# A mixture-of-experts stage between two attentions: when expert codes are read, rows are zeroed, outputs fetched and one batch staged

## What is computed

```python
    x = x + _L0_attn_ref(_layernorm(x, axis=-1), ...)
    x = x + _L0_xattn_ref(_layernorm(x, axis=-1), ctx_1024, ctx_1024, ...)
    x = x + _L0_ffn_ref(_layernorm(x, axis=-1), ...)    # mixture of experts
    x = x + _L1_attn_ref(_layernorm(x, axis=-1), ...)
    x = x + _L1_xattn_ref(_layernorm(x, axis=-1), ctx_1024, ctx_1024, mask_1xSxS2_ff0, ...)
    x = x + _L1_ffn_ref(_layernorm(x, axis=-1), ...)

def _L0_ffn_ref(x, gate_w, gate_b, w1, b1, w2, b2):
    gate_logits = jnp.einsum('bsd,de->bse', x, gate_w) + gate_b
    weights, indices = jax.lax.top_k(gate_logits, TOP_K)          # 2 of 8 experts
    weights = jax.nn.softmax(weights, axis=-1)
    h = jnp.einsum('bsd,edh->ebsh', x, w1) + b1[:, None, None, :]
    xh, gh = jnp.split(h, 2, axis=-1)
    act = jax.nn.silu(gh) * xh
    out_e = jnp.einsum('ebsf,efd->ebsd', act, w2) + b2[:, None, None, :]
    ...
    return jnp.sum(sel * weights[..., None], axis=2)
```

## Time and profile before

| | us |
|---|---|
| median of 3 runs | 814.25 (810.34 to 815.94) |
| the profiled execution, its own time | 816.3 |
| its span, first to last instruction | 814.5 |
| busy in the span: PE, VectorE, ScalarE, GpSimd | 691.9, 554.0, 412.8, 287.2 |
| outputs of the tiles (y_sb), first and last start | 370.7 to 512.5 |
| mean granted clock of TensorE | 0.875 of full speed |

### The profile page before, as it was taken

One profiled execution on the slowest core, in us unless ns is written; L12 is line 12 of the kernel. 1 busy time (PEld: TensorE's weight loads), 2 busy tenths in 40 slices (PEclk: granted clock), 3 DMA queues, 4 the chain that ended last, 5 costly groups with the idle time before them and its releaser, 6 DMA issues.

```text
span 814.5 us, 16187 instructions
## 1 busy us (share of the span) xinstructions
PE 691.9 (85%) x5016; PEld 377.3 (46%) x5021; DVE 554.0 (68%) x1674; ACT 412.8 (51%) x787; POOL 287.2 (35%) x509
## 2 busy tenths in 40 slices
PE   2768999999989999558699897788899989997987
PEld 1334455454434454348599896222232323334543
DVE  3757678787745556637357584797798998943564
ACT  1322565656664544213233354165787777784544
POOL 5732444554551204373123242235233241341310
PEclk9785999999985756759899999588999999999899
DMA  7552443254222311227457767220222101000000
GB/s 220 163 180 84 144 116 109 74 175 157 70 79 69 90 43 50 91 84 209 137 168 227 246 183 257 71 92 27 93 102 94 53 28 53 2 2 1 13 14 27
DMA packets 77252, 83.45 MB, mean 102 GB/s; under 512 B 15040, under 2 KB 67712, under 8 KB 77168
## 3 DMA queue, kind: packets, MB, share of 16 engines
q1 hardware_dynamic: 74896, 77.72, 31.0%
q0 software_dynamic: 2272, 4.69, 1.6%
HBM read 53.99 MB, written 28.00 MB: 101 GB/s over the span
## 4 chain that ended last, share of the span: by engine, by line
PE 58%; DVE 19%; issue 8%; DMA 5%; ACT 3%; SPq 3%; POOL 2%; DVEq 0%; ACTq 0%; POOLq 0%
PE bank_pv L743 12%; DVE mx L603 10%; PE bank_turn L587 8%; PE bank_scores L1827 6%; PE bank_scores L2161 5%; PE bank_scores L695 4%; PE bank_scores L1835 3%; PE bank_turn L762 3%; DMA probs<-routed_tokens 2%; PE bank_turn L804 2%; PE bank_turn L541 2%; DVE stats L463 1%; PE bank_turn L591 1%; PE bank_turn L592 1%; PE bank_scores L1238 1%
## 5 line engine op out<-in xcount | busy, mean ns | idle before, releaser
L603 DVE TENSOR_REDUCE mx<-bank_turn 128x1 f32<-128x512 f32 (+3 forms) x451 | 259.8, 615 | 58.8 <-PE bank_turn L592 31.8
L587 PE MATMUL bank_turn<-stk 64*128 64x77 bf16 (+4 forms) x707 | 166.2, 316 | 29.3 <-DVE mx L603 21.4
L695 PE MATMUL bank_scores<-stk 64*128 64x512 bf16 (+4 forms) x576 | 179.1, 376 | 5.3 <-ACT probs L716 4.0
L720 ACT ACTIVATE probs<-bank_scores 128x1024 f32<-128x1024 f32 (+4 forms) x160 | 117.0, 768 | 109.2 <-PE bank_scores L695 109.0
L716 ACT ACTIVATE probs<-bank_scores 128x512 f32<-128x512 f32 x256 | 138.9, 605 | 37.7 <-PE bank_scores L695 36.9
L743 PE MATMUL bank_pv<-probs,vsl 128*32 128x512 f32 (+4 forms) x1152 | 146.5, 583 | 2.7 <-POOL probs L728 1.8
L587 PEld LDWEIGHTS bank_turn<-stk 64*128 64x128 bf16 x707 | 54.7, 102 | 135.3 <-DVE mx L603 70.8
L1827 PE MATMUL bank_scores<-probs,w 128*128 128x128 f32 x624 | 88.7, 293 | 7.6 <-issue 5.1
L1827 PEld LDWEIGHTS bank_scores<-probs,w 128*128 128x128 f32 x624 | 83.2, 208 | 9.4 <-issue 9.1
L1886 ACT ACTIVATE probs<-bank_scores,b_cols 128x128 f32<-128x128 f32 x156 | 44.6, 368 | 82.0 <-PE bank_scores L1827 81.8
L728 POOL TENSOR_SCALAR_AFFINE_SELECT probs<-probs 128x256 f32<-128x256 f32 x128 | 51.8, 408 | 75.5 <-ACT probs L720 74.2
(11 more groups left out here) (289 smaller groups left out, 988.1 us busy)
## 6 DMA issues: line engine op xcount, KB each, us to landing
w<-in_M_w SPq DMA_DIRECT2D x43, 512.0 KB, 4.4
stk<-stack_A SPq DMA_DIRECT2D x64, 256.0 KB, 3.1
stack_A<-parts SPq DMA_DIRECT2D x16, 384.0 KB, 3.1
stack_A<-fill SPq DMA_DIRECT2D x8, 512.0 KB, 5.2
stack_A<-parts SPq DMA_DIRECT2D x16, 256.0 KB, 3.2
stk<-stack_X SPq DMA_DIRECT2D x16, 256.0 KB, 2.7
probs<-routed_tokens SPq DMA_DIRECT2D x39, 65.0 KB, 2.7
stack_A<-parts SPq DMA_DIRECT2D x16, 128.0 KB, 3.2
```

The source lines that it names most:

```text
L587: mm = e.matmul(o, stk[r, slot, 0, pp, qt * P:(qt + 1) * P], stk[r, slot, 1, pp, 0:keys], start=True, stop=not a.causal)
L603: e.tensor_reduce(o.rearrange("p h q -> p q h"), bank_of((g, m))[:, 0:k * keys].rearrange("p (q h k) -> p q h k", q=len(tiles), h=len(hs)) ...
L695: mm = e.matmul(score_bank(g, kt, i)[0:a.kp, 0:S - q0], stk[r, slot, 1, pp, kt * P:kt * P + a.kp], stk[r, slot, 0, pp, q0:S], start=True, ...
L720: e.activation(probs[0:a.kp, probs_of(g, kt), j:HG:2, 0:n], bank_scores[0:a.kp, 2 * j:2 * j + 2, 0:n], ACT.Exp, scale=1 / math.sqrt(HD)).t ...
```

## The change

It alters where things stand in the five lists; no product and no byte of data is added or left out, but the splitting of batch 1 goes to other engines.

1. `codes` becomes `expert_of`: each engine reads one word where the first tile of its four needs it. It is still 11 reads on each engine.
2. SyncE writes one zero row block after each of tiles 1 to 8 instead of all eight between tiles 1 and 2.
3. The outputs of batches 0 and 1 are fetched from ScalarE's queue, after silu of tile 26 (`fetch_sp` becomes `fetch_dma`).
4. Batch 1 is no longer projected and split beside the tiles. Its combining and normalising stand at tiles 33 to 35; its transposing and projecting stand between the maxima of unit 32 in the second stream, and GpSimd splits q ahead of `neg_of(32)` and k behind it. Batch 0's splitting is spread over tiles 30 to 33, its part 3 made at tile 32 instead of 33, and its `stack_dma` stands after tile 36 instead of 37. Beside tiles 37 and 38 stand 2 maxima each instead of 3, all of them behind `output(37)`, and the fourth bank is free from the start of the second stream.
5. GpSimd writes row blocks 4 and 5 ahead of the norm of batch 2, and 6 and 7 ahead of the norm of batch 3.

```diff
@@ -1407,11 +1401,13 @@
             neg_of(e, 1)
             for g in STREAMS[0]:
                 unit_pool(e, g)
-            norm_pool(e, M0.ln, 2)
             for t in range(QT, QT + 2):
                 scatter_pool(e, t)
+            norm_pool(e, M0.ln, 2)
+            for t in range(QT + 2, 2 * QT):
+                scatter_pool(e, t)
             norm_pool(e, M0.ln, 3)
-            for t in range(QT + 2, NT):
+            for t in range(2 * QT, NT):
                 scatter_pool(e, t)
 
         def first_stream_sp(e):
@@ -1428,12 +1424,21 @@
                 unit_sp(e, g)
 
         def second_stream_pe(e):
+            away[3] = 0
             for k in range(2 * MAXIMA_BESIDE, len(A1.items)):
                 max_pe(e, 32, k)
+                if k == 2 * MAXIMA_BESIDE:
+                    norm_pe(e, A1.ln, 1)
+                elif k % 3 == 0 and k < len(A1.items):
+                    z = (k - 6) // 3
+                    for part in range(2):
+                        if z < 2:
+                            stage_q_pe(e, A1, 1, z, part)
+                        elif z == 2:
+                            stage_v_pe(e, A1, 1, part)
             turn_pe(e, 32)
             for k in range(len(A1.items) // 2):
                 max_pe(e, 33, k)
-            away[3] = 0
             for g in STREAMS[1]:
                 unit_pe(e, g)
             last_layers_pe(e)
@@ -1444,19 +1449,26 @@
             turn_dve(e, 32)
             for k in range(len(A1.items) // 2):
                 max_dve(e, 33, k)
-            part31_dve(e, 1)
             for g in STREAMS[1]:
                 unit_dve(e, g)
             last_layers_dve(e)
 
         def second_stream_act(e):
+            norm_act(e, A1.ln, 1)
+            for z in range(2):
+                stage_q_act(e, A1, 1, z)
+            stage_v_act(e, A1, 1)
             for g in STREAMS[1]:
                 unit_act(e, g)
             last_layers_act(e)
 
         def second_stream_pool(e):
             values_pool(e, 32)
+            for step in range(4):
+                split_pool(e, A1, 1, 0, step)
             neg_of(e, 32)
+            for step in range(4):
+                split_pool(e, A1, 1, 1, step)
             bias_pool(e, A1, 0)
             bias_pool(e, A1, 1)
             for end in (0, S + 1):
...
@@ -1712,18 +1722,16 @@
                     moments_dve(e, A1.ln, 0)
                 elif t == 28:
                     normalise(e, A1.ln, 0)
-                elif t == 29:
+                elif t == 30 or t == 31:
+                    rest1_dve(e, 0, t - 30)
+                elif t == 32:
+                    part31_dve(e, 0)
+                elif t == 33:
                     combine_dve(e, 2, 1)
-                elif t == 30:
+                elif t == 34:
                     moments_dve(e, A1.ln, 1)
-                elif t == 31:
-                    rest1_dve(e, 0)
-                elif t == 32:
+                elif t == 35:
                     normalise(e, A1.ln, 1)
-                elif t == 33:
-                    part31_dve(e, 0)
-                elif t == 36:
-                    rest1_dve(e, 1)
                 elif t > 36:
                     for k in range(MAXIMA_BESIDE * (t - 37), MAXIMA_BESIDE * (t - 36)):
                         max_dve(e, A1.first, k)
@@ -1737,19 +1745,22 @@
             e.wait_ge(m["recip"], 1)
             e.tensor_tensor(gate[:, 1], gate[:, 0], gate_t[:, 1], ALU.mult).then_inc(m["gates"], 1)
 
-        MAXIMA_BESIDE = 3
+        MAXIMA_BESIDE = 2
 
         def place_in(t):
 
             return t if t < EARLY else LATE_AT + t - EARLY
 
-        def codes(e, late):
-
-            e.wait_ge(m["tile_e"], CODED * (1 + late))
-            words = range(LATE_AT // CODED, SLOTS // CODED) if late else range(LATE_AT // CODED)
-            code = {c: e.value_load(tile_e[0:1, c:c + 1], min_val=0, max_val=NE ** CODED - 1) for c in words}
-            tiles = range(EARLY, BUSY_TILES) if late else range(EARLY)
-            return {t: (code[place_in(t) // CODED] >> (3 * (place_in(t) % CODED))) & (NE - 1) for t in tiles}
+        def expert_of(e, ex, t):
+
+            k = place_in(t)
+            if k % CODED == 0:
+                e.wait_ge(m["tile_e"], CODED * (1 + (k >= LATE_AT)))
+                code = e.value_load(tile_e[0:1, k // CODED:k // CODED + 1], min_val=0, max_val=NE ** CODED - 1)
+                for n in range(CODED):
+                    if place_in(t + n) == k + n:
+                        ex[t + n] = (code >> (3 * n)) & (NE - 1)
+            return ex[t]
 
         def combine_dve(e, ln, b):
 
@@ -1858,14 +1868,10 @@
                     norm_pe(e, A1.ln, 0)
                 elif t == 30:
                     stage1_pe(e, 0)
-                elif t == 33:
-                    norm_pe(e, A1.ln, 1)
-                elif t == 34:
-                    stage1_pe(e, 1)
-                elif t > 35:
-                    if t == 36:
+                elif t > 36:
+                    if t == 37:
                         away[:3] = 3 * taken
-                    for k in range(MAXIMA_BESIDE * (t - 36), min(MAXIMA_BESIDE * (t - 35), MAXIMA_BESIDE * 2)):
+                    for k in range(MAXIMA_BESIDE * (t - 37), MAXIMA_BESIDE * (t - 36)):
                         max_pe(e, A1.first, k)
             e.wait_ge(m["y_out"], FREE + BUSY_TILES)
 
...
+            ex = {}
             for t in range(BUSY_TILES):
-                if t == EARLY:
-                    ex |= codes(e, 1)
                 gate_part(t, ex)
-                if t == 30:
+                if t == 26:
+                    for b in range(2):
+                        fetch_dma(e, b)
+                elif t == 30:
                     norm_act(e, A1.ln, 0)
                 elif t == 31:
                     stage1_act(e, 0, 0)
                 elif t == 32:
                     stage1_act(e, 0, 1)
+                    stage1_act(e, 0, 2)
                 elif t == 33:
-                    stage1_act(e, 0, 2)
+                    stage_v_act(e, A1, 0)
                     stage1_act(e, 0, 3)
-                elif t == 34:
-                    norm_act(e, A1.ln, 1)
-                elif t == 35:
-                    stage1_act(e, 1, 0)
-                elif t == 36:
-                    stage1_act(e, 1, 1)
-                    stage1_act(e, 1, 2)
-            stage1_act(e, 1, 3)
 
         def moe_sp(e):
             def tile(t):
@@ -1920,48 +1920,47 @@
                     e.wait_ge(m["y_at"], t - 1)
                 e.dma_start(x_in[:, t % 2], scr_xn[bass.ds(row, P), :]).then_inc(m["tile_in"][t % 2], 16)
 
-            def weights(t, ex):
+            def weights(t):
+                n = expert_of(e, ex, t)
                 wait(e, m["plain_half"], t - W_SLOTS + 1)
-                e.dma_start(w_now[:, t % W_SLOTS], d["M0_w"][bass.ds(ex[t], 1)].rearrange("a p n -> p (a n)"))\
+                e.dma_start(w_now[:, t % W_SLOTS], d["M0_w"][bass.ds(n, 1)].rearrange("a p n -> p (a n)"))\
                     .then_inc(m["w_in"][t % W_SLOTS], 16)
 
+            def zeros(n):
+                if n == 0:
+                    e.wait_ge(m["zero_at"], 1)
+                row = e.value_load(zero_row[0:1, n:n + 1], min_val=0, max_val=DEAD - P)
+                e.dma_start(scr_xn[bass.ds(row, P), :], pads[:, n]).then_inc(m["zeros"], 16)
+
+            ex = {}
             e.wait_ge(m["zeroed"], 2)
             e.dma_start(scr_xn[DEAD:DEAD + 2 * P, :].rearrange("(n p) d -> p n d", p=P), pads[:, NE:PADS])\
                 .then_inc(s_zero, 16)
-            ex = codes(e, 0)
             for t in range(W_SLOTS):
-                weights(t, ex)
+                weights(t)
             e.wait_ge(s["pv"], chunk0[2 * UN])
             e.wait_ge(m["scattered"][0], 16 * 2 * NT // 2)
-            for t in range(2):
-                tile(t)
-            e.wait_ge(m["zero_at"], 1)
-            for n in range(NE):
-                row = e.value_load(zero_row[0:1, n:n + 1], min_val=0, max_val=DEAD - P)
-                e.dma_start(scr_xn[bass.ds(row, P), :], pads[:, n]).then_inc(m["zeros"], 16)
-            for t in range(2, EARLY):
+            for t in range(EARLY):
                 tile(t)
                 if t >= W_SLOTS:
-                    weights(t, ex)
-            ex |= codes(e, 1)
-            weights(EARLY, ex)
+                    weights(t)
+                if t > 0:
+                    zeros(t - 1)
+            weights(EARLY)
             e.wait_ge(s_zero, 16)
             e.wait_ge(m["zeros"], 16 * NE)
             e.wait_ge(m["scattered"][1], 16 * 2 * NT // 2)
             for t in range(EARLY, BUSY_TILES):
                 tile(t)
                 if t > EARLY:
-                    weights(t, ex)
-                if t == 28:
-                    for b in range(2):
-                        fetch_sp(e, b)
-                elif t == 37:
+                    weights(t)
+                if t == 36:
                     for z in range(2):
```

(2 more changed lines are left out.)

44 lines of the change are left out of this document (17 added, 27 removed).

## The result

The changed kernel takes 789.77 us (median of 5 runs, 789.07 to 795.67) where the kernel before takes 815.66 (5 runs beside it, 810.34 to 815.96): ratio 0.9728, 95% interval 0.9686 to 0.9770. The forecast was 792. The profiled execution is the longest of the five, 795.67, against 816.3 before: 20.6 us less.

The account below looks back on a forecast made before the run. PE bounds undisturbed tiles at 2.84 us each, so gains lie where PE waits. Terms -4.5 - 11.7 - 2 - 4.9 + 1 = -22.1 took the 814.25 us median to 792; range 782 to 803.

Parts of the forecast that it names:

- Start: First tiles: reads no longer block VectorE and PE (3.95 us), tile 2 in time (0.57); -4.5, bounds -2 to -5.5.
- Tiles 7 to 10: Single reads end the serial waits; tile 9 still about 1.7 us late for zero blocks; -11.7, bounds -13.4 to -8.
- Fetches: Fetches from ScalarE's queue let the tile go ahead, though transfers are shared; -2, bounds -4.3 to +1.
- Tiles 33 to 38: Batch 1's projections and waits go; new 4.1 us wait at tile 37, 0.8 slower clock; -4.9, bounds -9 to -1.
- Behind the tiles: Second stream: more maxima and batch 1's staging, part 3 dropped, q's splitting covered; +1, bounds -0.7 to +4.
- Reads that stand open on PE: In the tile loop, PE's nine later words cost 0.65 us each, 5.9 us: 798; chance 0.11.
- The tail gives it back: Tile 37's wait grows, tail gains nothing, `neg_of(32)` waits behind q's splitting at half clock: 800; chance 0.14.
- No new waits: Tiles 9 and 37 arrive in time, another 1.7 + 4.9 us: 785; chance 0.08.
- The slower case: Four engines' reads fall in series for each of nine words and the clock falls: +16, 830; chance 0.05.

Follow-up runs that it names:

- b_reads: Kernel before with only the single reads (`expert_of` in place of `codes`) on all four engines: 798.64 us, ratio 0.9852.
- b_reads_zeros: Kernel before with the single reads and one zero block behind each of tiles 1 to 8, nothing else: 796.80 us, ratio 0.9789.
- a_scatter_old: Changed kernel with GpSimd's scatters in the order of before: 791.98 us, ratio 0.9751.
- a_stack_act: Changed kernel with batch 0's six stack DMAs issued by ScalarE, q's behind tile 34 and k's behind tile 35: 790.28 us, ratio 0.9714.
- 39 reads: Changed kernel with TensorE reading the word ahead of every output, 39 reads instead of 11: 792.06 us, ratio 0.9777.
- combined kernel: Changed kernel with zero blocks behind tiles 1 to 6, stack DMAs on ScalarE behind tiles 34 and 35, fetches behind tiles 26 and 29: 786.87 us, ratio 0.9735.
- a_stack_split: Changed kernel with q's three stack DMAs behind tile 36 and k's three behind tile 37: 794.01 us, ratio 0.9811.
- a_fetch_sp: Changed kernel with the two fetches back on SyncE's queue behind tile 28: 795.83 us, ratio 0.9794.

## Why the prediction was right, and where it was not

The forecast of 792 was off by 2.2 us, and the measured ratio on the 814.25 that it started from is 792.1. But the terms don't come out as well as their sum. They add up to -22.1; the two profiles differ by 20.6, of which 3.2 lie upstream of the change (from 200 to 330 us TensorE is busy for 121.0 us before and for 117.7 after), so what the terms describe measured -17.4. That the medians fell by as much as forecast is in part luck of the executions, and no run here says how large that part is. Point by point:

**Start, -4.5: measured -4.9.** The size was right, the split was not. (With the 2.04 us of half speed at 357.35, which only one other kernel with the change has, it is -4.9; in the other eight it is -5.8 to -6.1, beyond my bound.) I gave 3.95 to the reads and 0.57 to tile 2, as what each showed open in the old profile. Alone, the reads bring 0.2 (b_reads): tile 2 had been late all the time, behind a wait that covered it. The zero rows bring another 3.2, and the last 1.5 is tile 0's earlier turning (15.6 instead of 17.1 behind the mark in b_reads_zeros), whose cause stays open. It came right because the change does both. The scatters in the old order cost nothing in a_scatter_old, so they only make room, as said, or spare the spread named there.

**Tiles 7 to 10, -11.7: measured -8.6.** Here a step failed: "an estimated 2 us until the last block has landed". It took 3.5: issued at 378.31, and SyncE's next read at 381.90. Tile 9's wait was 2.90 instead of 1.7, and the half clock behind it, which I had kept for the bound, came too: 16.2 less the 11.5 at pace is 4.7, 2.90 of waiting and 1.8 of half speed. The other end that I had named for that landing, a tile's 3.9, would have given -9.8 before the clock. And b_reads shows that the reads alone remove the whole -13.3; the interleaved zero rows are what takes 4.7 of it back.

**Fetches, -2: measured -0.6.** Inside the bounds, and with a wide spread: in the other kernels that issue both fetches there the stretch is 1.2 to 2.5 us shorter than before. That from ScalarE's queue "the tile goes ahead of them" was right, and the danger named beside it was the one that came: VectorE's combining waits for the fetched rows, 1.85 us against 0.41 before, where I had allowed about 1 us more, and the copy behind it keeps TensorE waiting as long as before. Issued by ScalarE, then, the rows' landing takes the gain, not the weights'. What I missed is that 7.5 us is the floor, set by VectorE's 2.18 us of combining ahead of the copy, and that the fetches leave the stretch anywhere between that and 11.2. The Trainium skill's rule (Trainium Kernel Development and Optimization, Key Constraints: queues share the 16 DMA engines, another queue saves issue time) agrees with both cases: the weights' landing of 6.71 us beside fetches from another queue, and a_stack_act, where moving 4.71 us of issuing to an idle engine gave 3.0 us.

**Tiles 33 to 38, -4.9: measured -4.6.** The new wait is at tile 37, behind the six DMAs, as forecast: 2.85 us instead of 4.1. What fills the difference is a wait that I had not listed, 0.93 us at 473.67, behind VectorE's combining of batch 1, and the half speed behind tile 37's wait: 22.2 less 17.0, 2.85 and 0.93 leaves 1.4 us for it, where I gave 0.8.

**Behind the tiles, +1: measured +1.4** to the first exponential, and the same in every kernel: 15.3 with the staging beside the tiles, 16.7 to 17.0 without. The number is luck. I took it between two clocks, -0.7 at full speed and more at half; from 488 to 500 us the granted clock was 1.00 (0.50 before), and still it was +1.4. VectorE does not bound this stretch alone, as I had it: it makes its 14 maxima in 9.9 us, not 8.5, and waits three times for TensorE, whose maxima stand behind the staging (0.41, 0.41 and 0.38 us), as here:

```profile
493.61 1.89 DVE L603 TENSOR_REDUCE mx<-bank_turn 128x1 f32<-128x512 f32 x3 [0.41 <-PE bank_turn L587]
```

`neg_of(32)` so starts 10.4 us behind tile 38's output instead of 8.3, and 0.7 us come back between it and the exponential. The 1.28 us of part 3 that I took off brought nothing: before, it stood at 527.04, behind the maxima of both units. The splitting on GpSimd is covered, as said. Moving batch 1's staging out is thus worth 3.8 us in 32-38 (b_reads against the changed kernel) and costs 1.4.

**Rivals.** Reads that stand open on PE: refuted by 39 reads, and with them that result of the floor for a `tensor_load` in the Trainium skill (DMA: Bandwidth & Descriptors, Latency and other measured facts). Grouping saved nothing to be seen here: the reads of a block follow each other in 0.53 us (ScalarE) to 0.65 us (TensorE), and the blocks fell in series. "The tail gives it back" is refuted for its mechanism: with and without tile 37's wait the tail is 16.7 to 17.0 us, and `neg_of(32)` waited for the last maximum, not for q's splitting. "No new waits" would have needed the combined kernel's placing. The slower case never showed.

## What to carry to other kernels

Short register reads belong singly in front of waits that the engine has anyway, not in a block in front of everything: the block puts one engine's reads behind another's. An idle time in a profile is the price of the last cause alone; look at when the next operand was ready before giving each cause its share. And for a load that gates others, count from its issue to its landing, 3.5 us here under load, and compare times on both engines, not tile numbers.

## What the runs showed of the hardware

TensorE's list up to the mark at L785 is the same in all kernels, and the profiled executions reached the mark between 331.9 us (a_stack_split) and 339.9 us (a_scatter_old). The windows of TensorE from 200 to 330 us of these two kernels, in that order, differ in the granted clock and hence in the busy time:

```profile
200.00:330.00 130.00, 113.78 (x912) 0.78 0.23 66
```

```profile
200.00:330.00 130.00, 121.12 (x902) 0.70 0.22 63
```

That is of the size of the 10 us by which executions of one kernel differ (the kernel before: 806.31 us at a mean clock of 0.888, 816.99 at 0.869), and it lies ahead of everything that was edited but the order of the scatters. A wait of 2.96 us of TensorE in tiles 26 to 28 was followed by matmuls at half speed in a_fetch_sp (8 in 1.92 us) and by matmuls at full speed in the changed kernel (8 in 1.13); what decides between them no run here settles.
